# Moving layer 1's keys, values, queries and context sums into the attention's batches, with edge columns in fours and a front by groups of two tiles

## What is computed

```python
xn = _layernorm(x, axis=-1)
x = x + _L1_gnn_ref(xn, edge_index, ...) + _L1_mix_ref(xn[None], ...)[0]
# graph attention, 8 heads of 64
h = jnp.einsum('ni,hio->nho', x, W)
e = s_src[src] + s_tgt[tgt]; e = jnp.where(e >= 0, e, 0.2 * e)
ex = jnp.exp(e - m[tgt]); denom = segment_sum(ex, tgt)
out = segment_sum(h[src] * (ex / (denom[tgt] + 1e-16))[:, :, None], tgt) @ Wo + bo
# linear-attention mixer, 8 heads of 32
q = elu(x @ Wq.T) + 1; k, v = elu(x @ Wk.T) + 1, x @ Wv.T
context = einsum('bhnd,bhne->bhde', k, v); k_sum = k.sum(axis=2)
out = (einsum(q, context) / max(q . k_sum, 1e-6)) @ Wproj.T + bproj
```

## Time and profile before

| | |
|---|---|
| median of 3 runs | 2208.18 us (2205.98 to 2212.14) |
| profiled execution, span first to last instruction | 2202.1 us |
| its own time | not given apart; the three runs are 2212.14, 2205.98 and 2208.18 |
| mean granted TensorE clock | 0.957 of 2.4 GHz |
| TensorE, VectorE, ScalarE, GpSimd busy | 89%, 62%, 34%, 48% of the span |
| layer 0's gather and mixer | 328 to 824 us |
| layer 1's front | 1079 to 1217.8 us |
| layer 1's attention | 1217.8 to 1673.5 us |

### The profile page before, as it was taken

One profiled execution on the slowest core, in us unless ns is written; L12 is line 12 of the kernel. 1 busy time (PEld: TensorE's weight loads), 2 busy tenths in 40 slices (PEclk: granted clock), 3 DMA queues, 4 the chain that ended last, 5 costly groups with the idle time before them and its releaser, 6 DMA issues. The chain is left out here.

```text
span 2202.1 us, 31834 instructions
## 1 busy us (share of the span) xinstructions
PE 1970.5 (89%) x9640; PEld 1293.1 (59%) x9640; DVE 1364.2 (62%) x2895; ACT 738.7 (34%) x1951; POOL 1053.7 (48%) x1094
## 2 busy tenths in 40 slices
PE   8999947989898986799789598888889899999999
PEld 3455523544444445799656476766767756656565
DVE  7696528887888766333385698988988821221111
ACT  4422211212121213344343565555552332333322
POOL 5688867777777620333250677777773400000000
PEclk9999978999999997899899799999999999999999
DMA  4144423333334314422231888888885000000000
GB/s 136 27 130 109 128 68 109 104 105 102 102 102 101 94 32 155 145 72 71 77 109 44 238 243 239 241 238 241 240 233 151 1 1 10 1 10 1 10 10 9
DMA packets 116896, 233.41 MB, mean 106 GB/s; under 512 B 27615, under 2 KB 71782, under 8 KB 114038
## 3 DMA queue, kind: packets, MB, share of 16 engines
q0 software_dynamic: 53808, 151.72, 24.7%
q1 hardware_dynamic: 62918, 79.64, 11.3%
HBM read 190.44 MB, written 40.68 MB: 105 GB/s over the span
## 5 line engine op out<-in xcount | busy, mean ns | idle before, releaser
L2465 PE MATMUL p_ag<-rows_g,oh_g 128*128 128x260 f32 x1408 | 381.9, 412 | 58.9 <-issue 42.5
L2216 POOL DMA_INDIRECT rows_g<-g_table,row_src x352 | 333.4, 947 | 166.3 <-issue 102.0
L894 POOL DMA_INDIRECT rows<-h_table,row_rel x352 | 339.5, 965 | 125.7 <-issue 101.6
L2465 PEld LDWEIGHTS p_ag<-rows_g,oh_g 128*128 128x128 f32 x1408 | 246.0, 194 | 87.4 <-issue 61.9
L2831 DVE SCALAR_TENSOR_TENSOR x<-p_yf,cw_f,x 128x256 f32<-128x256 f32 (+1 forms) x160 | 66.4, 477 | 278.6 <-PE p_yf L2991 278.6
L380 POOL DMA_INDIRECT slot_table<-rec_f,dst_i x140 | 181.9, 1299 | 41.7 <-issue 41.7
L2322 DVE TENSOR_TENSOR rows_g<-rows_g,p_e 128x2048 f32<-128x2048 f32 x88 | 200.3, 2276 | 0.0
L1192 PE MATMUL p_agg<-rows,oh 128*128 128x256 f32 x624 | 159.7, 394 | 1.1 <-DVE x L951 1.1
L1030 DVE TENSOR_TENSOR fT<-a_sb,p_sel 128x512 f32<-128x512 f32 x200 | 128.1, 682 | 30.6 <-PE p_sel L1244 30.4
L2991 PE MATMUL p_yf<-f,h_f 128*128 128x256 f32 (+1 forms) x640 | 145.7, 381 | 0.8 <-ACT h_f L2883 0.8
L2941 PE MATMUL p_1f<-qT,f 128*128 128x512 f32 (+1 forms) x320 | 142.4, 588 | 0.5 <-ACT qT L2859 0.5
(11 more groups left out here) (499 smaller groups left out, 3499.4 us busy)
## 6 DMA issues: line engine op xcount, KB each, us to landing
h_table<-h_out SPq DMA_DIRECT2D x20, 1024.0 KB, 4.4
where_g<-d_table SPq DMA_DIRECT2D x88, 128.0 KB, 4.1
w<-in_L_ffn_W SPq DMA_DIRECT2D x16, 512.0 KB, 9.8
y_table<-yb_g SPq DMA_DIRECT2D x47, 128.0 KB, 1.7
rows<-h_table,row_rel POOLq DMA_INDIRECT x352
rows_g<-g_table,row_src POOLq DMA_INDIRECT x352, 4.2
g_table<-row SPq DMA_DIRECT2D x20, 260.0 KB, 2.1
f<-in_L_ffn_W SPq DMA_DIRECT2D x16, 256.0 KB, 6.4
```

The costliest lines, as they stand in the source:

```text
L894: pool.indirect_dma_start(rows[:, r, j], None, st.h_rows, bass.IndirectOffsetOnAxis(ap=st.row_rel[:, at:at + 1], axis=0)).then_inc(gathere ...
L2216: pool.indirect_dma_start(rows[:, r, j], None, st.g_table, bass.IndirectOffsetOnAxis(ap=st.row_src[:, at:at + 1], axis=0)).then_inc(gather ...
L2465: last = pe.matmul(p_a[:, k % NS, h, 0:HALF], oh[:, r, j], rows[:, r, j, h * HALF:(h + 1) * HALF], start=j % w == 0, stop=j % w == w - 1)
```

## The change

Three things are done together.

1. Columns in fours. A batch now is one of three kinds (`WIDTH`): 69 batches with one unit of four columns, nine with two units of two, ten with four units of one. The 19 narrow ones stand at batches 4, 8, ..., 76, singles at 4, 12, ..., 76, pairs at 8, 16, ..., 72. That makes 127 units and as many adds in each pass and as many copies in `nodes`. The number of columns, gathers and products is the same. `slots_and_front` works out the new map: about six more constants on GpSimd, one more prefix product, four or five more steps of VectorE. The attention's PSUM ring of units falls from three to two.

2. `front1` makes only the scores' product and the rows `h`. The two weight loads still go out at its start, but are waited for in `attend`. The normalisation moves to ScalarE, after VectorE has made `lift` = -mean/std; the turned tile is kept in `st.qT`. Work goes by groups of two tiles (the first two and the last two alone) and `p_q` and `p_h` have two buffers. There is no exponential in this stage any more.

3. `attend` makes keys, values, queries and context sums. For each two tiles there is a span of eight batches: TensorE makes keys and values of a tile after the second and fourth column of batches 0 and 3 of a span, the context of a tile after those of batches 4 and 7, and the queries of both tiles after each column of batch 6. Keys and values and queries share one PSUM bank (`p_q = p_kv`). ScalarE takes keys and values in its iterations 2 and 5 of a span, and the queries at the end of iteration 8, which is the first of the next span; VectorE makes the features an iteration later. The last eight batches have none of this.

```diff
-PAIRED = (-(-E // P) - T) // BATCH
-NSINGLE = NBATCH - PAIRED
-SINGLE_AT = [4 + (NBATCH // NSINGLE) * i for i in range(NSINGLE)]
-assert SINGLE_AT[-1] < NBATCH
-FIRST_COLUMN = [(PAIRED + SINGLE_AT.index(s)) * BATCH if s in SINGLE_AT else (s - sum(a < s for a in SINGLE_AT)) * BATCH
-                for s in range(NBATCH)]
+NEED = -(-E // P)
+QUADS = -(-(NEED - T * (BATCH - 1)) // BATCH)
+PAIRED = (NEED - T) // BATCH - QUADS
+SINGLE = NBATCH - QUADS - PAIRED
+NARROW = PAIRED + SINGLE
+NARROW_AT = [NBATCH // NARROW * (i + 1) for i in range(NARROW)]
+assert NARROW_AT[-1] < NBATCH and SINGLE in (PAIRED, PAIRED + 1)
+WIDTH = [(SUP if NARROW_AT.index(s) % 2 else 1) if s in NARROW_AT else BATCH for s in range(NBATCH)]
+CLASS_AT = {BATCH: 0, SUP: QUADS, 1: QUADS + PAIRED}
+FIRST_COLUMN = [(CLASS_AT[w] + WIDTH[:s].count(w)) * BATCH for s, w in enumerate(WIDTH)]
...
+            def add_group(k, done, tiles):
+                dve.wait_ge(agg_done, done)
                 if k:
                     dve.wait_ge(agg_added, k)
-                for n, tile in enumerate(mine):
+                for n, tile in enumerate(tiles):
                     out = st.x[:, ds(tile * D, D)]
                     last = dve.tensor_tensor(out, out, p_agg[:, k % 3, n * D:(n + 1) * D], ALU.add)
-                    if n + 1 < len(mine):
+                    if n + 1 < len(tiles):
                         link(last)
                 last.then_inc(agg_added, 1)
 
             def first_sum(s, tiles):
-                if s:
-                    add_sum(GR * (s - 1), tiles)
+                if s and WIDTH[s - 1] == BATCH:
+                    add_group(GROUP[s - 1], GR * s, tiles)
+                elif s:
+                    add_group(GROUP[s - 1], GR * s - 1, tiles[:len(tiles) // GR])
+
+            def second_half(s, tiles):
+                if s and WIDTH[s - 1] < BATCH:
+                    add_group(GROUP[s - 1] + 1, GR * s, tiles[len(tiles) // GR:])
...
-            sp.dma_start(w_kv[:, :, :], io["wkv1"].rearrange("(k p) o -> p k o", p=P)).then_inc(w_in, 16)
-            sp.dma_start(w_q[:, :, :], io["wq1"].rearrange("(k p) o -> p k o", p=P)).then_inc(w_in, 16)
+            sp.dma_start(st.w_kv1[:, :, :], io["wkv1"].rearrange("(k p) o -> p k o", p=P)).then_inc(st.w_kv_in, 16)
+            sp.dma_start(st.w_q1[:, :, :], io["wq1"].rearrange("(k p) o -> p k o", p=P)).then_inc(st.w_kv_in, 16)
...
+                dve.scalar_tensor_tensor(out=lift[:, lo:hi], in0=mean[:, lo:hi], scalar=-1.0, in1=rstd[:, lo:hi],
+                                         op0=ALU.mult, op1=ALU.mult).then_inc(rstd_ready, 1)
...
+            def take(t):
+                dve.wait_ge(q_ready, t + 1)
                 if t >= 2:
-                    dve.wait_ge(transposed, t - 1)
-                dve.tensor_scalar(xn[:, t % 2], st.x[:, t * D:(t + 1) * D], mean[:, t:t + 1], rstd[:, t:t + 1],
-                                  ALU.subtract, ALU.mult).then_inc(xn_ready, 1)
...
-            def take(t):
-                u = t % 2
-                dve.wait_ge(kv_ready, t + 1)
-                if t:
-                    dve.wait_ge(exp_ready, t)
-                if t >= 2:
-                    dve.wait_ge(c_ready, t - 1)
-                dve.tensor_scalar(neg[:, u, 0:D], p_kv[:, u, 0:D], 0.0, None, ALU.min)
...
+                    dve.wait_ge(row_stored[t % 2], 16 * (t // 2))
+                dve.tensor_copy(row[:, t % 2, HF:], p_q[:, t % 2, 0:H])
...
+            for n, (lo, hi) in enumerate(GROUPS):
+                for t in range(lo, hi):
+                    add_back(t)
+                measure(lo, hi)
+                if n:
+                    for t in range(*GROUPS[n - 1]):
+                        take(t)
                 invert(n)
-                norm(n)
-            for t in range(T):
-                take(t)
-                for u in ADDED[t][0:1]:
-                    add_back(u)
-                features(t)
-                for u in ADDED[t][1:]:
-                    add_back(u)
-                starting = FIRST.get(t + 2)
-                if starting is not None:
-                    measure(*GROUPS[starting])
-                    invert(starting)
-                if t + 2 < T:
-                    norm(t + 2)
+            take(T - 1)
...
+            def norm(t):
+                if t >= XN:
+                    act.wait_ge(transposed, t - XN + 1)
+                nc.scalar.activation(xn[:, t % XN], st.x[:, t * D:(t + 1) * D], ACT.Identity, bias=lift[:, t:t + 1],
+                                     scale=rstd[:, t:t + 1]).then_inc(xn_ready, 1)
...
+            for n, (lo, hi) in enumerate(GROUPS):
+                deviation(n)
+                act.wait_ge(rstd_ready, n + 1)
+                for t in range(lo, hi):
+                    norm(t)
+                for t in range(lo, hi):
+                    take_x(t)
+                if n:
+                    for t in range(*GROUPS[n - 1]):
+                        take_h(t)
+            take_h(T - 1)
...
+            for n, (lo, hi) in enumerate(GROUPS):
+                for t in range(lo, hi):
+                    pe.wait_ge(xT_ready, t + 1)
+                    halves = [st.qT[:, t * D + k * P:t * D + (k + 1) * P] for k in range(K)]
+                    if t >= 2:
+                        pe.wait_ge(s_taken, t - 1)
                     for k in range(K):
-                        pe.matmul(p_q[:, c * P:(c + 1) * P], w_q[:, k, c * P:(c + 1) * P], halves[k], start=k == 0, stop=k == K - 1)
-                for k in range(K):
-                    last = pe.matmul(p_q[:, D:D + 2 * H], halves[k], w_a[:, k], start=k == 0, stop=k == K - 1)
-                last.then_inc(q_ready, 1)
-                if t + 1 < T:
-                    turn(t + 1)
-                if t:
-                    context_product(t - 1)
-                if t:
-                    pe.wait_ge(h_copied, t)
-                for k in range(K):
-                    last = pe.matmul(p_h[:, :], halves[k], w_h[:, k], start=k == 0, stop=k == K - 1)
-                last.then_inc(h_ready, 1)
-            context_product(T - 1)
+                        last = pe.matmul(p_q[:, t % 2, 0:2 * H], halves[k], w_a[:, k], start=k == 0, stop=k == K - 1)
+                    last.then_inc(q_ready, 1)
+                    if t + 1 == hi and hi < T:
+                        for u in range(*GROUPS[n + 1]):
+                            turn(u)
+                    if t >= 2:
+                        pe.wait_ge(h_copied, t - 1)
+                    for k in range(K):
+                        last = pe.matmul(p_h[:, t % 2], halves[k], w_h[:, k], start=k == 0, stop=k == K - 1)
+                    last.then_inc(h_ready, 1)
...
-    NS = 3
+    NS = 2
...
+    SPAN = 8
+    KV_AT, CONTEXT_AT, Q_AT = (0, 3), (4, 7), 6
+    TAKE_KV, TAKE_Q = (2, 5), SPAN
...
+            def key_features(t):
+                dve.wait_ge(k_pos, t + 1)
+                dve.wait_ge(k_exp, t + 1)
+                dve.tensor_tensor(k_f[:, t % 2], k_f[:, t % 2], k_e[:, :], ALU.add).then_inc(k_made, 1)
+
+            def query_features(m):
+                dve.wait_ge(q_pos, m + 1)
+                dve.wait_ge(q_exp, m + 1)
+                q = st.qT[:, m * 2 * D:(m + 1) * 2 * D]
+                dve.tensor_tensor(q, q, q_e[:, :], ALU.add).then_inc(q_made, 1)
+
+            def behind(s):
+                m, phase = divmod(s - 1, SPAN)
+                if m < T // 2 and phase in TAKE_KV:
+                    key_features(2 * m + TAKE_KV.index(phase))
+                m, phase = divmod(s - 1 - TAKE_Q, SPAN)
+                if 0 <= m < T // 2 and phase == 0:
+                    query_features(m)
...
+            def take_kv(t):
+                act.wait_ge(kv_done, t + 1)
+                if t >= 2:
+                    act.wait_ge(c_done, t - 1)
+                if t:
+                    act.wait_ge(k_made, t)
+                nc.scalar.activation(k_e[:, :], p_kv[:, 0:D], ACT.Relu, scale=-1.0).then_inc(k_low, 1)
+                nc.scalar.activation(k_f[:, t % 2], p_kv[:, 0:D], ACT.Relu).then_inc(k_pos, 1)
+                v = p_kv[:, D:].rearrange("p (c e) -> p c e", c=2)
+                if t == T - 1:
+                    nc.scalar.copy(v_m[:, t % 2, :, P:], st.rowmask[:, 0:1].unsqueeze(1).broadcast_to([P, 2, 1]))
+                    nc.scalar.activation(v_m[:, t % 2, :, 0:P], v, ACT.Copy, scale=st.rowmask[:, 0:1]).then_inc(v_taken, 1)
+                else:
+                    nc.scalar.copy(v_m[:, t % 2, :, 0:P], v).then_inc(v_taken, 1)
+                act.wait_ge(k_low, t + 1)
+                nc.scalar.activation(k_e[:, :], k_e[:, :], ACT.Exp, scale=-1.0).then_inc(k_exp, 1)
+
+            def take_q(m):
+                act.wait_ge(q_done, m + 1)
+                if m:
+                    act.wait_ge(q_made, m)
+                nc.scalar.activation(q_e[:, :], p_q[:, :], ACT.Relu, scale=-1.0).then_inc(q_low, 1)
```

(94 more changed lines are left out.)

231 lines of the change are left out of this document (104 added, 127 removed).

## The result

The changed kernel takes 2223.32 us (median of four runs, 2220.91 to 2225.77) against 2207.1 for the kernel before (four runs). The ratio is 1.0068, with a 95% interval of 1.0053 to 1.0084: slower by 0.7%. The profiled execution took 2221.83 us, its span 2220.1.

A forecast was written before the change was run, and what follows sets the result against it. GpSimd's gather issue, 4.98 us per batch of four columns, was taken to bound the attention. Terms 0.5-9-46+56 = +1.5 us moved the span from 2202.1 to 2203.6, median 2210 us; range 2168 to 2238.

The forecast's parts named there:

- Prelude: Before layer 0: more constants, one tiny product and five chained VectorE steps cost +0.5 us (0 to +2).
- Layer 0: Gather and mixer: fewer adds save 0.4 us in each of 22 TensorE waits for VectorE, -9 us (-3 to -25).
- Rival D: Layer 0 gains its waits for VectorE, -25 us, net -14.5, 2194 us; chance 0.06.
- Front: Layer 1's front: moved products and normalisation shorten it, attention starts at 1172, -46 us (-36 to -52).
- The group period of 6.7: Layer 1's front: a group of two tiles takes 6.3 us, 6.7 with hand-overs and two row buffers awaiting stores.
- Attention: Layer 1's attention: TensorE's inserted products, stalls at the shared bank and clock loss add +56 us (+43 to +70).
- the clock's term: Attention: TensorE products at half speed after each shared-bank stall cost 1.3 us a stall (0 to 1.7).
- The attention near 512 us: Sign for the forecast: attention stage near 512 us; under 485 or over 530 would show it wrong.
- Rival C: Attention: each stall halves TensorE's clock for two batches, 49.5 us a later span, net +33, 2241 us; chance 0.14.
- Rival B: Attention: ScalarE reaches the take earlier, hardly any stall, span 42 us, net -35, 2173 us; chance 0.18.
- Rival F: Attention: inserted products fit TensorE's 73 us to spare, GpSimd's pace stays, net -54, 2154 us; chance 0.05.
- Rival E: Front: GpSimd's clears hold VectorE through the measure, groups meet badly, front -38, net +9.5, 2218 us; chance 0.07.

The follow-up runs named there:

- The move alone: The change's front and attention with the old column map (196 adds, ring of two units), against the kernel before: 2255.57 us, ratio 1.0242.
- the fours alone: New column map and adds, with the front and attention products of the kernel before and a ring of three: 2197.88 us, ratio 0.9968.
- the measure's other form: On the take at 7, two scalar steps of layer 1's measure get a second SBUF operand: 2172.86 us, ratio 0.9858 to the kernel before.
- the take at 7: The changed kernel, but ScalarE takes the queries at the end of iteration 7 of a span, not 8: 2175.37 us, ratio 0.9875 to the kernel before.
- the stalls at 1.29: The changed kernel, with ScalarE taking the queries before its node copies in iteration 8 of a span: 2197.07 us, ratio 0.9968 to the kernel before.
- the early scores: On the take at 7, VectorE makes the next batch's scores and turned one-hots before a single-column batch's adds: 2163.31 us, ratio 0.9806.
- all of it: The take at 7, the early scores, the measure's other form and four row buffers together: 2151.04 us, ratio 0.9749 to the kernel before.

## Why the prediction was right or wrong

The span moved by +18.0 where +1.5 was the sum. The median, 2223.32, is inside the range of 2168 to 2238 and over the 0.3% that was called no change; it stands 3.2 above its span where I had added 6.1. The direction had stood at 0.33, behind faster with 0.43, and the range went from 1.8% faster to 1.4% slower, so that the time fell into it says little. The parts also covered for one another: the attention alone was 18.4 over its forecast, and 6 us that layer 0 and the stage behind it gave beyond theirs hid a third of that.

Prelude: +0.5 forecast, +2.4 measured (the first gather of layer 0 starts at 330.9 instead of 328.5), just over the bound. That start lies between 329.4 and 331.2 in the eight kernels with the new map, at 328.5 and 328.3 in the two with the old.

Layer 0: -9 forecast, -11.0 measured. The step was right as made: PE's wait for DVE's `kx` fell from 21.6 us in 22 waits to 14.5 in 14, and all waits ahead of that product from 27.2 to 17.9. The move alone, with the old map, takes 463.5 us from first to last product and the fours alone 455.3, against 464.4 and 453.4 before and after, so most of the gain is the map's. Rival D (-25) falls. Route and experts behind it, which the change leaves alone, came out 4.2 shorter. They take 266.6 to 268.3 us in the eight executions with the new map and 271.0 and 269.7 in the two with the old, so it seems to go with the map; why stays open.

Front: -46 forecast, -43.7 measured from the experts' gather to the first aggregation product. The group period of 6.7 was 6.9 (POOL's gathers of a group began at 1094.58, 1101.51 and 1108.45). For the clears 3 us were charged; the step was held for 5.4, but by the measure's other form no more than 1.7 of it reached the group. The row buffers cost more than the 0.4 a group that I added: with four of them the front is 6.9 shorter than in the change.

Attention: +56 forecast, with +70 as the upper bound, +74.4 measured. **This is the step that failed.** The mechanism held to the tenth: the place (the product after the second column of batch 8m+8), the number (nine) and the length (3.43 for 3.4) of the stall. The size that was off is the clock's term, "1.3 a stall (0 to 1.7)": every stall brought a half clock, and it cost 2.7 on average (1.6 once, 2.7 to 2.9 eight times), which is 12.6 us more than charged and lies outside the term's own bound. I had taken it from gaps of 1.9 us and mixed in gaps that cost nothing; a stall of 3.4 is longer than any gap of the earlier trace rows, and the bound had to reach beyond them. The other 6 us: a span without stall or half clock takes 41.65 and not 41.3, which is 3 over nine spans, and two half clocks behind single-column batches, 1.65 each, had no term at all (one of them is in the first span, 45.9 where 44.3 were forecast).

The length of a gap would not have given the size by itself. The kernel before has one wait of 3.15 us that the earlier trace rows lacks, and no half clock followed it:

```profile
1613.07 1.11 PE L2465 MATMUL p_ag<-rows_g,oh_g 128*128 128x260 f32 x4 [3.15 <-DVE rows_g L2322]
...
1614.10 1.12 PE L2465 MATMUL p_ag<-rows_g,oh_g 128*128 128x260 f32 x4
```

"The attention near 512 us" meant the stage from its first gather; from there to the last product it went from 454.8 to 528.7, where 510.8 was due and over 530 was named as the sign of being wrong. That the aggregation products alone took 511.4 is a coincidence. The first gather came at 1161.8 and not near 1172; the forecast's own terms for prelude and layer 0 put it at 1163.5.

Rival C had this mechanism. The text said that it decides from a loss of 1.9 us a stall; at 2.7 its condition was met, and by the text's own arithmetic the change had to come out slower. So the threshold fits and the chance of 0.14 looks too low; the size C names, 49.5 us a span, was 47.9. (C's sum gives an attention of +87.2, not +87.5.) Rival B (the stall is hardly there) is what the take at 7 builds: a ratio of 0.9875 measured, 2173/2208.18 = 0.984 forecast. Rival F falls: POOL waits 79.9 us for PE. Rival E's hold is real and cost little. The rule of the Trainium skill on the shared ports ("SBUF — State Buffer", section "Who interferes with whom") is borne out for a step of two elements a partition; steps with two SBUF inputs, the reciprocal and the copies out of PSUM ran beside the clears. The hold was not for one GpSimd instruction alone: the step began in the ninth of the twenty clears, 0.55 us each, and ended with the twentieth.

## What to carry to other kernels

Work moved from a stage that it bounds into the slack of another is worth what the other stage's waits leave, so the order of a helper engine's iteration decides: here one iteration's offset of an ACT pass was worth 2% of the kernel. When a stall lands on TensorE and TensorE has become the bound, charge the clock too, with an upper bound above what shorter gaps have cost: the same trace can show gaps that cost nothing. Before giving up a move that came out even or slower, list what its bounding engine waits for: the stall at the bank held 51 of the attention's 74.4 us, and the wait after the single-column batches another 10.

## What was not expected of the hardware

Identical gaps do not cost the same: PE's wait of 1.93 us after a single-column batch brought a half clock twice in ten in the changed kernel, four times in ten once the long stalls were gone, and eight times in ten with the stalls at 1.29. Length alone does not order them: 1.71 and 1.81 us brought one, 3.15 us did not. What else decides, these runs do not settle. Waits of 1.11 and 1.29 us brought none in 29 cases (nine of 1.29, twenty of 1.11 in the early scores and in all of it); the stalls of 3.4 to 3.7 us brought one in all nine cases of the change and all nine of the move alone, with the clock back sooner in one and in six of them.

A tensor-scalar step over only two elements a partition is held by GpSimd's clears until the last of them ends, as a wide one is: 5.36 us, where the same step took 0.17 ahead of the clears, at 1125.31.
